# VectorE's three register loads for four items: in a row at the end of the edge loop's body, or at three places of it

## The reference

```python
def _L3_gnn_ref(node_emb, edge_index, W1, b1, W2, b2, Wg, bg):
    src, dst = (edge_index[0], edge_index[1])
    pair_emb = jnp.concatenate([node_emb[src], node_emb[dst]], axis=-1)
    h = jax.nn.relu(pair_emb @ W1 + b1)
    interaction = h @ W2 + b2
    gate = jax.nn.sigmoid(interaction @ Wg + bg)
    gated = interaction * gate
    N = node_emb.shape[0]
    summed = jax.ops.segment_sum(gated, src, num_segments=N)
    counts = jax.ops.segment_sum(jnp.ones((src.shape[0],), dtype=gated.dtype), src, num_segments=N)
    return summed / jnp.maximum(counts, 1.0)[:, None]
```

## Time and profile before

| | |
|---|---|
| median of 3 runs | 3859.66 us (3855.13 to 3863.49) |
| the profiled execution's own time | 3853.53 us |
| its span in the trace | 3851.8 us |
| PE busy | 3108.9 us, 81% of the span |
| DVE busy | 2702.2 us, 70% |
| ACT busy | 1951.9 us, 51% |
| POOL busy | 1615.6 us, 42% |

### The profile page before, as it was taken

One profiled execution on the slowest core, in us unless ns is written; L12 is line 12 of the kernel. 1 busy time (PEld: TensorE's weight loads), 2 busy tenths in 40 slices (PEclk: granted clock), 3 DMA queues, 4 the chain that ended last, 5 costly groups with the idle time before them and its releaser, 6 DMA issues.

```text
span 3851.8 us, 144496 instructions
## 1 busy us (share of the span) xinstructions
PE 3108.9 (81%) x46724; PEld 2623.8 (68%) x46725; DVE 2702.2 (70%) x7781; ACT 1951.9 (51%) x4306; POOL 1615.6 (42%) x1691
## 2 busy tenths in 40 slices
PE   5986246777888869989989867778999999999996
PEld 2443123433444459889879867777999999999996
DVE  9998989999999950420320276666777777777777
ACT  7975035777888830000000033336666666666665
POOL 1000068468777774057777620003333333333331
PEclk9987568988999989999999967778999999999998
DMA  1000022222233269899889657774333333333332
GB/s 49 5 3 1 11 86 98 92 104 84 102 108 112 102 250 338 285 317 318 308 265 312 205 169 248 249 246 125 96 97 94 97 96 95 96 97 96 94 97 67
DMA packets 219825, 550.28 MB, mean 143 GB/s; under 512 B 67881, under 2 KB 129573, under 8 KB 193855
## 3 DMA queue, kind: packets, MB, share of 16 engines
q1 hardware_dynamic: 161315, 480.18, 36.8%
q0 software_dynamic: 51616, 66.64, 6.7%
q10 hardware_dynamic: 6716, 1.12, 0.2%
HBM read 400.09 MB, written 151.85 MB: 143 GB/s over the span
## 4 chain that ended last, share of the span: by engine, by line
PE 56%; DVE 21%; issue 11%; DVEq 6%; ACT 4%; DMA 1%; POOL 1%; ACTq 0%; SPq 0%; PEldq 0%; POOLq 0%
PE ps L2089 17%; DVE x L636 10%; PE ps L2284 8%; PE ps L2064 8%; PE ps L2296 8%; PE ps L2250 7%; DVE rows L762 6%; PE ps L2275 3%; PE ps L2264 2%; ACT stage L1784 1%; DVE x L1068 1%; DVEq L1060 1%; DVEq L1057 1%; PE ps L2007 1%; DVEq L1056 1%
## 5 line engine op out<-in xcount | busy, mean ns | idle before, releaser
L2064 PE MATMUL ps<-rows 128*128 128x448 bf16 x2272 | 632.6, 411 | 220.9 <-DVE rows L762 155.3
L1548 POOL DMA_INDIRECT x<-b_rows_all,gidx x416 | 403.4, 970 | 785.6 <-DVE x L1068 655.9
L762 DVE TENSOR_SCALAR rows<-iota_c,x 128x448 bf16<-128x448 bf16 x2272 | 679.5, 373 | 15.1 <-PE ps L2064 14.2
L2064 PEld LDWEIGHTS ps<-rows 128*128 128x128 bf16 x2272 | 331.1, 146 | 522.4 <-issue 403.0
L1904 ACT ACTIVATE x<-ps,b1col 64x256 f32<-64x256 f32 x920 | 431.9, 469 | 391.6 <-PE ps L2275 331.2
L1452 POOL DMA_INDIRECT quad_keys<-key_quads,key_at x416 | 451.9, 1086 | 127.3 <-issue 126.5
L1784 ACT ACTIVATE stage<-ps 128x448 bf16<-128x448 f32 x700 | 385.5, 554 | 205.5 <-PE ps L2064 196.5
L2284 PE MATMUL ps<-w2cat,x 128*128 128x128 f32 x3680 | 487.2, 276 | 0.0
L2089 PE MATMUL ps<-x,rows 128*128 (+1 forms) x13230 | 419.2, 195 | 60.2 <-issue 39.8
L1501 POOL DMA_INDIRECT dst_ids<-ids,slot x416 | 411.0, 988 | 126.8 <-issue 126.8
L2296 PE MATMUL ps<-x 128*128 128x65 f32 x3680 | 462.2, 269 | 0.1
(11 more groups left out here) (406 smaller groups left out, 4068.9 us busy)
## 6 DMA issues: line engine op xcount, KB each, us to landing
rows<-adjacency SPq DMA_DIRECT2D x90, 1024.0 KB
adjacency<-stage SPq DMA_DIRECT2D x50, 1568.0 KB
x<-adjacency SPq DMA_DIRECT2D x60, 1024.0 KB
b_rows_all<-x SPq DMA_DIRECT2D x116, 512.0 KB, 3.5
x<-src_rows SPq DMA_DIRECT2D x460, 128.0 KB, 3.1
rows<-adjacency SPq DMA_DIRECT2D x90, 544.0 KB
x<-adjacency SPq DMA_DIRECT2D x60, 544.0 KB
x<-dst_ids SPq DMA_DIRECT2D x116, 256.0 KB, 4.3
```

The lines of the kernel that those rows point to most:

```text
L762: ins = e.tensor_scalar(hot_dst[:, k, :], iota_c[:], rel_col[:, bass.ds(i0 + k, 1)], None, ALU.is_equal)
L1548: e.indirect_dma_start(out=BGT[:, s, :, :].rearrange("p j f -> p (j f)"), out_offset=None, in_=b_rows_all, in_offset=bass.IndirectOffsetOn ...
L2064: e.matmul(psf[:, bass.ds(at_bank, WIN)], hot_src[:, k // HOTS, :, k % HOTS], hot_dst[:, k % HOTS, :], start=False, stop=False, skip_group ...
```

## The change

`load_slots` loaded two of the tables; it is split, so that each of the three tables has a function of its own. In the loop's body the load of the groups' numbers (L1056) moves up to s = 3, between `add_b` and `make_hot_t`. The load of the tiles (L1060 before, L1062 after) moves to s = 0 of the round that uses it, between `make_hot_t` and `gated`, so the one ahead of the loop falls away. The load of the slots (L1057 before, L1059 after) stays at the body's end. The number of loads in a round is three before and after, and nothing that computes is changed.

```diff
+            def load_groups(at):
+                e.load(item_groups, group_tab[0:1, bass.ds(at, 4)])
+
             def load_slots(at):
-                e.load(item_groups, group_tab[0:1, bass.ds(at, 4)])
                 e.load(item_slots, slot_tab[0:1, bass.ds(at, 4)])
...
             e.wait_ge(total_zeroed, 1)
             e.sem_inc(sum_taken, 1)
+            load_groups(0)
             load_slots(0)
             load_tiles(4)
             for i in range(8):
                 if i >= 2:
                     add_b(i - 2, (i - 2) % 4)
                 if i % 4 == 3:
+                    load_groups(i + 1)
                     load_slots(i + 1)
...
-            load_tiles(8)
             with e.Fori(2, ITEMS // 4) as r:
                 for s in range(4):
                     i = 4 * r + s
                     add_b(i - 2, (s + 2) % 4)
+                    if s == 3:
+                        load_groups(i + 1)
                     make_hot_t(i, r, s, False)
+                    if s == 0:
+                        load_tiles(i)
                     gated(i - 4, s % 2, False)
                     add_sum(i - 5, (s + 1) % 2, s)
                     make_hot(i - 1, (s + 3) % 4, False)
                 load_slots(4 * r + 4)
-                load_tiles(4 * r + 4)
```

## The result

The changed kernel takes 3767.57 us (median of 4 runs, 3763.97 to 3772.44), the kernel before 3861.57 us (4 runs, 3855.13 to 3870.14). The ratio is 0.9756, with a 95% interval of 0.9733 to 0.9779: 94.0 us less. The profiled span is 3766.8 us instead of 3851.8.

The account below looks back on a forecast made before the run. TensorE was taken as nearly the bound, losing 0.84 us a round waiting for add_b. All of it was to come back: 113 rounds by 0.84 us is 94.9 us, so 3859.66 - 94.9 = 3765 us, range 3756 to 3790.

Parts of the forecast that it names:

- The bound, and the size of the stall: Edge stage: TensorE nearly the bound, its transposes waiting for add_b once a round; 0.84 us lost in each of 113 rounds.
- The way at the end of the body: Body's end: with two loads gone, add_b starts 0.91 us earlier and the transposes are in time by 0.06 us.
- s = 3: Between add_b and make_hot_t: a load of 0.45 us fits into VectorE's existing waiting; make_hot_t later by 0 to 0.3 us.
- The size of the cover: At s = 3, between add_b and add_sum: VectorE's waiting for ACT and TensorE's sums, 0.45 us, hides the load.
- The reason given for a cheap load: Ahead of the loop, two loads between add_b and make_hot_t cost 0.15 us because the sequencer ran ahead of the engine.
- s = 0: Between make_hot_t and gated: add_b to add_b at most 2.30 us against 2.38, gated at most 1.05 against 1.16.
- Nothing of the stall stayed: Rival at the round's late step: 0.1 to 0.5 us a round would stay, 3776 to 3822 us; chance 0.17.
- the gap did not move to ACT or POOL: Rival in the edge stage: TensorE would wait for ACT or the gather instead, 3860 us, no change; chance 0.04.
- a load does not wait for what its engine computes: Rival claiming the opposite, in mid-item and at the body's end: loads wait for VectorE's computing, 3884 us; chance 0.03.
- x = 0.35 us: Hold ahead of each mid-item load from which waiting for the engine's computing would lose more than the change gains.
- the margin of 0.06 us: Body's end: transposes ready at 3220.41 us, where TensorE wants them at 3220.47.
- the 3810 us by the page's price: Load left at body's end at 0.8 us for four registers: transposes 0.40 us late a round, gain only 50 us.

Follow-up runs that it names:

- half changes: Against the kernel before, only the groups' or only the tiles' load moved, the other left at the body's end: 3801.48 and 3802.85 us.
- e10: Changed kernel plus a fourth load a round with used registers (second set of slots) at the body's end: 3796.59 us, ratio to before 0.9837.
- e6: Changed kernel with the slots' load moved behind the groups' load at s = 3, none at the body's end: 3762.78 us, ratio to before 0.9763.
- e9: Changed kernel plus a fourth load with used registers (second set of tiles) at s = 0, behind the tiles' load: 3777.64 us, ratio to before 0.9795.
- e11: Kernel before plus a fourth load a round with used registers (second set of slots) at the body's end: 3898.3 us, ratio 1.0109.
- e12: Changed kernel plus a fourth load with used registers (second set of tiles) at s = 0, behind gated: 3775.02 us, ratio to before 0.9801.
- e1: Against the changed kernel, the tiles' load put back at the body's end, only the groups' load moved: 3801.48 us, ratio to before 0.9846.

## Why the prediction was right, point by point
**The bound, and the size of the stall.** One late step in each round, 0.84 us by 113 rounds, was forecast as 94.9 us; the medians differ by 94.0 and the stages by 94.0 us. Forecast were 3765 us, measured 3767.57.

**The way at the end of the body.** `add_b` was forecast to be 0.06 us early; it is 0.08 us. That is the smallest number of the case and the one that decided it. The half changes and e10 confirm it to 0.02 us: each lost its load less this margin (0.35 and 0.39 us, where 0.45 - 0.08 = 0.37, and 0.28, where 0.375 - 0.08 = 0.295).

**s = 3.** The wait for ACT and the sums covered the load: `gated` and `add_sum` start 1.85 and 2.32 us after the transposes of the item, 1.84 and 2.31 before. The load asked less of it than its 0.45 us, as forecast (0 to 0.3 us): `make_hot_t` starts 0.58 us after `add_b` instead of 0.34, 0.24 later. The size of the cover, forecast as 0.45 us, is measured in e6: `make_hot_t` is 0.69 us later there than with no load, but `add_sum` only 0.25 us (1.63 us after `add_b` instead of the 1.38 of the earlier trace rows), so 0.44 us were absorbed.

The reason given for a cheap load does not carry over from item 7, though. There two loads cost 0.15 us together, because the first started at 2636.74, 0.34 us ahead of `add_b`. In the loop of the changed kernel it starts at 3217.85, 0.11 us after `add_b` (0.05 to 0.12 us in 106 rounds). The sequencer has no lead over `add_b` there; one load is partly hidden under the 0.42 us that `add_b` itself takes, and the second load of e6 adds its full 0.45 us.

**s = 0.** `add_b` to `add_b` is 2.17 us; at most 2.30 were forecast. `gated` starts 0.86 us after `add_b`, at most 1.05 were forecast. The limit worked out for the first, 2.38 us, took the way to the transposes as equal at every item. It is not (0.67 us against 0.57), so the slack here was 0.19 us in truth, where the same sum with 0.57 us gives 0.29. This did not touch the forecast of the change. It is why the forecast for e9 was half of what was measured. At its full cost (2.30 us) the load would have left 0.06 us of the 0.19.

**The rivals.** Nothing of the stall stayed; the gap did not move to ACT or POOL; and a load does not wait for what its engine computes, since the one at s = 3 starts 0.11 us after `add_b`, which runs for 0.42 us, and lasts 0.344 us as ever. Two side sums of the prediction do not come out, and the forecast rests on neither. The turning point of that last rival, x = 0.35 us, counts the margin of 0.06 us twice; counted once it is (0.84 + 0.17 - 0.38) / 2 = 0.32 us. And the 3810 us by the page's price makes only the load at the end longer, not the two that move, so by that price the time would have been higher.

The price itself, about 0.8 us for four registers in the Trainium skill ("Runtime: NRT & Kernel Launch", "Instruction fetch mechanics"), is given there for the register loads that the runtime puts in. For this kernel's loads from SBUF the measurement decides: 0.343 us, and 0.375 us with all that belongs to it, as e11 measures.

## What to carry to other kernels
Where one engine sets the pace and another feeds it, price an instruction by its place: work out, item by item, how long before its consumer each signal comes, and put what costs sequencer time where that slack is largest; the number of instructions and the mean busy share say nothing about it. Measure the way from the signal to the consumer at each item too: one register operation on it took a third of the slack at s = 0. Check in the trace that an added instruction is there before reading its cost as nothing. And measure a stage by its own first and last instruction: here that repeated to 0.4 us, where the whole run scattered by 8 us and more.

## What the runs showed that was not expected
A gap of up to 0.18 us leaves no idle time in TensorE's records. In e12, PE is busy for all but 1.85 us of 1000 us, although 0.175 us is lost in each round, about 18 us in the same stretch (1000 / 9.70 rounds). The list of TensorE's waits has no entry in that stretch, and one in the whole stage:

```profile
2700.00:3700.00 1000.00, 998.15 (x12373) 989.85 (x12371) 846.51 (x3298) 696.72 (x1650) 355.84 (x374) 1.00 0.37 102
```

```profile
PE ps L2289 <- DVE x L1075: 1.0, 1, 1.0
```

The records of matmuls in a row overlap (two transposes of 0.27 us and more take 0.42 us together), and their ends are modelled. The larger gaps show 0.16 us less than is lost: 0.84 us lost shows as 0.68 idle, 0.36 in e1 as 0.20. The distance of starts is the measure, and the number of instructions in the stretch, 12373 against the changed kernel's 12615 in the same 1000 us, shows the loss too.
